# First layer of a four-layer image kernel: input rows in runs of 8192 bytes, single copies of shared rows, smaller steps, and row windows loaded for one group at a time instead of two

## What is computed

```python
def _gn(v, G=8, eps=1e-5):
    g = v.reshape(B_, G, C_ // G, H_, W_)
    ...
    return ((g - m) / jnp.sqrt(s + eps)).reshape(v.shape)
def _denoise_block(x, w1, b1, w2, b2, w3, b3, a, b, c):
    trip = _triplets(x)
    ...
    o = a * _conv_reflect(xf, w1, b1, 1, 2) + b * _conv_reflect(xf, w2, b2, 2, 4) + c * _conv_reflect(xf, w3, b3, 4, 8)
    return jnp.tanh(o).reshape(B, T, H, W)
y = _denoise_block(x, blk1_w1, ...)
z = _denoise_block(y, blk2_w1, ...)
return z
```

## Time and profile before

| | us |
|---|---|
| three runs | 5124.47, 5130.97, 5133.29 |
| the profiled execution | 5131.47 |
| its span | 5129.7 |
| TensorE busy | 4772.3 (93%) |
| VectorE busy | 4133.9 (81%) |
| ScalarE busy | 4039.3 (79%) |
| first group of layer 0 starts | 79.93 |
| last group of layer 0 starts | 2984.01 |

### The profile page before, as it was taken

One profiled execution on the slowest core, in us unless ns is written; L12 is line 12 of the kernel. 1 busy time (PEld: TensorE's weight loads), 2 busy tenths in 40 slices (PEclk: granted clock), 3 DMA queues, 4 the chain that ended last, 5 costly groups with the idle time before them and its releaser, 6 DMA issues. The chain is left out here.

```text
span 5129.7 us, 174298 instructions
## 1 busy us (share of the span) xinstructions
PE 4772.3 (93%) x74557; PEld 2805.2 (55%) x74557; DVE 4133.9 (81%) x7219; ACT 4039.3 (79%) x4023; POOL 1532.3 (30%) x1643
## 2 busy tenths in 40 slices
PE   4799999999999999999999979997776999999998
PEld 2344444445455795565566744434555566666665
DVE  5786786876867888888888868888999688888888
ACT  3576776776767888888888887876997799999897
POOL 0111111111113222222222100004776355555556
PEclk9899999999999999999999989998999999999999
DMA  8899899999978778788778769996886466666654
GB/s 220 224 246 261 249 266 255 248 259 252 247 211 236 221 217 240 230 221 248 220 229 243 216 235 324 323 325 236 308 309 247 114 150 153 150 153 150 153 150 119
DMA packets 501930, 1161.93 MB, mean 227 GB/s; under 512 B 59593, under 2 KB 60232, under 8 KB 468042
## 3 DMA queue, kind: packets, MB, share of 16 engines
q1 hardware_dynamic: 499000, 1148.40, 77.0%
q10 hardware_dynamic: 2162, 2.39, 0.2%
HBM read 678.71 MB, written 453.51 MB: 221 GB/s over the span
## 5 line engine op out<-in xcount | busy, mean ns | idle before, releaser
L702 PE MATMUL c_p<-c_w,wc 128*32 128x512 f16 x38912 | 2270.7, 380 | 53.5 <-DMA c_w<-xs 48.2
L702 PEld LDWEIGHTS c_p<-c_w,wc 128*32 128x32 f16 x38912 | 1239.7, 96 | 935.9 <-issue 42.7
L792 ACT ACTIVATE c<-c_w 64x2052 f16<-64x2052 f16 x512 | 984.7, 1923 | 87.3 <-DMA c_w<-xs 74.9
L778 ACT ACTIVATE c_t<-c_p,cbias,cscale 128x512 f32<-128x512 f32 x512 | 398.1, 777 | 541.2 <-PE c_p L702 538.6
L702 PE MATMUL c_p<-c_n,wc 128*32 128x512 f16 x8192 | 589.8, 381 | 20.4 <-DVE c_n L638 19.3
L1780 PE MATMUL f_P<-f_qh,f_wt 64*64 64x512 f16 x4608 | 545.7, 378 | 1.8 <-DVE f_t L1676 1.8
L1780 PE MATMUL f_P<-f_hl,f_wt 64*64 64x512 f16 x4608 | 545.3, 379 | 0.0
L884 POOL COPY c_y<-c_y 128x16 f16<-128x16 f16 x512 | 191.1, 401 | 1070.6 <-DVE c_y L609 1070.6
L794 ACT ACTIVATE c<-c_w 64x2052 f16<-64x2052 f16 x256 | 492.9, 1925 | 6.3
L1941 POOL TENSOR_TENSOR f_y<-f_y,f_x 128x512 f32<-128x512 f32 x256 | 330.8, 1292 | 449.4 <-DVE f_hl L1655 443.3
L1540 POOL TENSOR_TENSOR e_hl<-e_g,e_hl 128x2048 f16<-128x2048 f32 x63 | 257.2, 4083 | 608.4 <-ACT e_hl L1490 608.4
(11 more groups left out here) (275 smaller groups left out, 7681.6 us busy)
## 6 DMA issues: line engine op xcount, KB each, us to landing
d_x<-x SPq DMA_DIRECT2D x128, 1024.0 KB, 7.8
x<-d_x SPq DMA_DIRECT2D x128, 1024.0 KB, 5.1
ys<-c_y SPq DMA_DIRECT2D x576, 132.0 KB, 6.7
xs<-a_hl SPq DMA_DIRECT2D x70, 1056.0 KB, 10.1
a_x<-in_x SPq DMA_DIRECT2D x256, 256.0 KB, 7.1
a_x<-in_x SPq DMA_DIRECT2D x128, 512.0 KB, 5.0
x<-a_x SPq DMA_DIRECT2D x512, 128.0 KB, 5.3
f_x<-x SPq DMA_DIRECT2D x256, 256.0 KB
```

The costliest lines, as they stand in the source:

```text
L702: t = p.matmul(pg[32 * j:32 * j + 32, :], weights[:, var], source[:, j, at:at + NW], start=start, stop=stop, tile_position=(0, 32 * j))
L778: s.activation(tt_[n % 3][:, :], pp[:, n % 4, :], ACT.Tanh, bias=cbias[:, blk:blk + 1], scale=cscale[:, blk:blk + 1]).then_inc(c_act, 1)
L792: s.activation(twice[n % 2][64:128, :, PAD - 2:PAD - 1 + NW], w[0:64, :, PW + PAD + 1:PW + PAD + 2 + NW], ACT.Copy).then_inc(c_2b, 1)
```

## The change

- `load_x` brings one channel in one copy of 128 runs of 8192 bytes, so a partition now holds four neighbouring rows (before: four copies, runs of 2048 bytes). `store_xs` writes one channel per copy, as soon as that channel is ready.
- Pair 0 and pair 8 keep no second copies. Where a window needs them, `sources(p)` lists from where each slot is loaded: three sources for p = 0, two for p = 7, one for the others.
- `load` fills one group (four row sets) instead of two, with a semaphore for each group. The number of its copies in the first layer goes from 1008 to 2288.
- `v0`, `v3`, `hi`, `mirror`, `store_xs` work on one channel; the preparation of a pair takes six groups instead of four and begins two or three groups earlier. `p0` now follows a full group after the statistics, `p1_` sits early in its group.
- The weights of later layers are built in ten parts at groups 15 to 46 and two at 50 and 57.

The second sum has moved forward within its group, and both stand a group later against VectorE's steps. The core of the diff:

```diff
-        def n_xs(i):
-
-            return 16 * sum(2 + (r % 8 in (0, 7)) for r in range(i))
+        def inputs_stored(e, i):
+
+            e.wait_ge(a_sd, 32 * (i - (i > 1)))
+            if i > 1:
+                e.wait_ge(a_s1[0], 16)
+                e.wait_ge(a_s1[1], 16)
 
         def stored(e, u):
 
-            e.wait_ge(c_yd[u % 2], 16 * sum(8 + 4 * (place(r)[2] in (0, 7)) for r in range(u % 2, u, 2)))
+            e.wait_ge(c_yd[u % 2], 128 * (u // 2))
+
+        def sources(p):
+
+            outer = {0: [(0, (0,), 1, 0), (0, (1,), 0, 1)], 7: [(8, (0,), 8, 0), (8, (1,), 7, 1)]}
+            return outer.get(p, []) + [(p + 1, (0, 1), p + 1, 0)] * (p < 7)
 
         def at_edge(half, g):
 
-            return (half, g // 2) in ((0, 0), (1, 1))
+            return (half, g) in ((0, 0), (1, 3))
 
         def rows_in(e, u, g):
 
-            n = sum(1 + (place(r)[2] == 0) for r in range(u % 2, u + 1, 2))
-            e.wait_ge(c_ld[u % 2][g // 2], 16 * (3 + at_edge(u % 2, g)) * n)
+            n = sum(len(sources(place(r)[2])) for r in range(u % 2, u + 1, 2))
+            e.wait_ge(c_ld[u % 2][g], 16 * (3 + at_edge(u % 2, g)) * n)
 
...
-            return 64 * image + 4 + 7 * j + 2 * (i == 3) if i > 2 else -2
-
-        steps = {first_group(i) + z: (i, z) for i in range(2, NG) for z in range(4) if first_group(i) + z >= 0}
-        loads_x = {first_group(i - 2) + 4 + 2 * c: (i, c) for i in range(4, NG) for c in range(2)}
+            return 64 * image + 2 + 7 * j + (i == 3) if i > 2 else -3
+
+        steps = {first_group(i) + z: (i, z) for i in range(2, NG) for z in range(6) if first_group(i) + z >= 0}
+        parts_at = [15 + 7 * (z // 2) + 3 * (z % 2) for z in range(10)]
...
-                def v0(i):
-                    v.wait_ge(a_ld[i % 2], 128 * (i // 2 + 1))
-                    for j in range(8):
-                        v.bn_stats(ast[:, j, :], xin[i % 2][:, j // 4, 512 * (j % 4):512 * (j % 4) + 512]).then_inc(a_bn, 1)
-                    v.wait_ge(a_bn, 8 * (i + 1))
-                    mark["m", i] = ch.step(v, v.bn_aggr(am[:, 0, :], ast[:, :, :].rearrange("p a b -> p (a b)")))
+                def v0(i, c):
+                    v.wait_ge(a_ld[i % 2], 32 * (i // 2 + 1))
+                    for j in range(4):
+                        v.bn_stats(ast[:, 4 * c + j, :], xin[i % 2][:, c, 512 * j:512 * j + 512]).then_inc(a_bn, 1)
+                    if c:
+                        v.wait_ge(a_bn, 8 * (i + 1))
+                        mark["m", i] = ch.step(v, v.bn_aggr(am[:, 0, :], ast[:, :, :].rearrange("p a b -> p (a b)")))
 
                 def v1(i):
                     v.wait_ge(a_p, 2 * i + 1)
...
-                def channel_weights():
...
+                def channel_weights(part):
...
+                    if part == 0:
+                        v.wait_ge(w13_ld, 160)
+                        v.wait_ge(w13_p, 1)
+                        ch.step(v, v.tensor_copy(rp[:, :, :].rearrange("p j n -> p (j n)"), pq[:, 0:432]))
+                        ch.step(v, v.memset(qf[:, :, :], 0.0))
...
                     rows4 = buf[:, 4 * g:4 * g + 4]
+                    i, s = stage_of(n)
                     for di in (4, 0, 1, 7, 8):
+                        if s == 3 and di == 1:
+                            p1_(i)
                         for wl, xl in ((0, 0), (0, 1), (1, 0)):
                             four(wu[:, blk, wl, :, di], rows4, xl * PW + PAD + DX[di], start=(di, wl, xl) == (4, 0, 0))
-                    i, s = stage_of(n - 1)
-                    if s == 0:
+                    if s == 2:
                         p0(i)
-                    if s == 1:
...
                         i, st_ = stage_of(4 * u + g)
+                        if st_ == 3:
+                            root_step(s, a_v, mark["rt", i], a_rt, ve, sq)
                         if 4 * u + g + 1 < 8 * NU:
                             copies(4 * u + g + 1)
-                        if st_ == 2:
-                            root_step(s, a_v, mark["rt", i], a_rt, ve, sq)
-                        if (u, g) == (5, 2):
+                        if 4 * u + g == 50:
                             root_step(s, a_v, mark["sv"], w13_rt, c2b[:, 1:2], c2b[:, 2:3])
                         evict(u, g)
                         if u < NU:
                             high(u, g)
-                        if st_ == 2:
-                            hi(i)
+                        if st_ in (3, 4):
+                            hi(i, st_ - 3)
...
                 def load_x(i, channels=(0, 1)):
                     b, g = divmod(i, 8)
                     if i >= 2:
-                        e.wait_ge(a_lo, i - 1)
-                    for c, r in ((c, r) for c in channels for r in range(4)):
-                        e.dma_start(xin[i % 2][:, c, NW * r:NW * r + NW],
-                                    dram(x, ((b * NC + 2 * g + c) * NH + 16 * r) * NW, [[NW, 16], [64 * NW, 8], [1, NW]])).then_inc(a_ld[i % 2], 16)
-
-                def store_xs(i):
+                        e.wait_ge(a_lo, 2 * (i - 1))
+                    for c in channels:
+                        e.dma_start(xin[i % 2][:, c, :], dram(x, (b * NC + 2 * g + c) * NH * NW, [[4 * NW, 128], [1, 4 * NW]])).then_inc(a_ld[i % 2], 16)
+
+                def store_xs(i, c):
                     b, g = divmod(i, 8)
-                    e.wait_ge(a_pad, i + 1)
-                    for c, gp, slot in [(0, g, 1), (1, g + 1, 0)] + [(1, 0, 0)] * (g == 0) + [(0, 8, 1)] * (g == 7):
-                        e.dma_start(dram(xs, pair(b, gp, 0, slot), [[YP, 16], [64 * YP, 8], [16 * YP, 4], [1, RW]]),
-                                    halves_of(i)[c][:, :, :, :].rearrange("p r l w -> p r (l w)")).then_inc(a_sd, 16)
+                    e.wait_ge(a_pad, 2 * i + c + 1)
+                    e.dma_start(dram(xs, pair(b, g + c, 0, 1 - c), [[4 * YP, 128], [YP, 4], [1, RW]]),
+                                halves_of(i)[c][:, :, :, :].rearrange("p r l w -> p r (l w)")).then_inc(a_s1[c] if i == 1 else a_sd, 16)
 
                 def load(u, g):
 
                     blk, b, p, half = place(u)
-                    src, first, last = ys if blk else xs, (half, g) == (0, 0), (half, g) == (1, 2)
+                    src, first, last = ys if blk else xs, (half, g) == (0, 0), (half, g) == (1, 3)
                     if u >= 2:
-                        e.wait_ge(c_pe, 4 * (u - 2) + g + 2)
+                        e.wait_ge(c_pe, 4 * (u - 2) + g + 1)
                     elif u == 1 and g == 0:
                         e.wait_ge(a_v, mark["wc"])
                     if u < 2 and (first or last):
...
                         r = 16 * b + 2 * min(7, p + 1) + 2
                         stored(e, r)
                         stored(e, r + 1)
+                    elif u < 2:
+                        e.wait_ge(a_sd, 32)
+                        e.wait_ge(a_s1[0], 16)
                     else:
-                        e.wait_ge(a_sd, n_xs(8 * b + min(7, p + 1) + 1))
-                    f, n = int(first), 8 - first - last
-                    parts = [(0, 48, -4, f, n), (96, 8, -8, f, 8 - f), (112, 8, 20, 0, 8 - last)]
-                    parts += [(16, 40, 0, 0, 1)] * first + [(0, 40, -4, 7, 1)] * last
-                    for gp in (0, 1) if p == 0 else (p + 1,):
+                        inputs_stored(e, 8 * b + min(7, p + 1) + 1)
+                    f, n = int(first), 4 - first - last
+                    parts = [(0, 48, -4, f, n), (96, 8, -8, f, 4 - f), (112, 8, 20, 0, 4 - last)]
+                    parts += [(16, 40, 0, 0, 1)] * first + [(0, 40, -4, 3, 1)] * last
+                    for gp, slots, of, slot in sources(p):
                         for to, count, row, j, banks in parts:
-                            e.dma_start(win[half][to + gp % 2:to + 2 * count:2, 4 * g + j:4 * g + j + banks],
-                                        dram(src, pair(b, gp, 256 * half + 64 * g + 16 * j + row), [[RW, count], [16 * YP, banks], [1, RW]])).then_inc(c_ld[half][g // 2], 16)
+                            at = dram(src, pair(b, of, 256 * half + 64 * g + 16 * j + row, slot), [[(3 - len(slots)) * RW, count * len(slots) // 2], [16 * YP, banks], [1, RW]])
+                            first_p = to + gp % 2 + 2 * slots[0]
+                            e.dma_start(win[half][first_p:to + 2 * count:6 - 2 * len(slots), 4 * g + j:4 * g + j + banks], at).then_inc(c_ld[half][g], 16)
...
-                store_xs(0)
+                store_xs(0, 0)
+                store_xs(0, 1)
+                store_xs(1, 0)
                 load_x(2)
-                store_xs(1)
+                store_xs(1, 1)
                 for u in range(2):
-                    for g in (0, 2):
+                    for g in range(4):
                         load(u, g)
                 load_x(3)
...
-                        if s == 3:
-                            store_xs(i)
-                        if u + 2 < 2 * NU and not late and g % 2:
```

(55 more changed lines are left out.)

127 lines of the change are left out of this document (62 added, 65 removed).

## The result

The changed kernel takes 5208.35 us (median; 5198.64 to 5211.07) beside 5128.26 of the kernel before in the same session (5124.47 to 5133.29): ratio 1.0152, 95% interval 1.0135 to 1.017. The profiled execution took 5209.05 us, its span 5207.1. It is slower by some 80 us; forecast were 5151 and a range of 5045 to 5200.

The account below looks back on a forecast made before the run. TensorE was taken as the bound, busy 1387.8 of 1390 us in pass two. Terms -14 + 5.5 - 21 - 24 - 6 + 66 + 8 + 7 = +21.5, rounded to +20 on 5131.47, gave 5151 us; range 5045 to 5200.

Parts of the forecast that it names:

- the queue's terms: SyncE's queue, held about 0.70 us per window copy, lags at changes of image: +66, +8 and +7 us.
- rival A: The queue does not bind (copies hold it 0.55 us or less, or waits have slack): 5045 us, chance 0.25.
- Head, -14: Start of layer 0: earlier raw loads, stores and one-group windows start the first group at about 65.5 us, not 79.93.
- Groups 0 to 8, +5.5: Start of pass one: pair 3's raw load behind 78 window copies stops TensorE in group 5; group 8 near 139.5.
- Weights -21: Later layers' weights built in parts that fit beside a group, replacing two long VectorE blocks: -21 us.
- statistics -24: A full group between VectorE's result and `p0` removes TensorE's 24.2 us of waits for statistics: -24 us.
- waits for nothing shown -6: Weight loads waiting on "issue" near 1100 us, 11.4 us; about a tenth less traffic in pass one saves half: -6.
- Pass one: Late `ys` stores at three changes of image cost 11.5 us each, 34, against about 27 before: +7 us.
- Into pass two, +8: Passage into pass two (groups 248 to 260): the residual of group 264 comes some 6 us late, +8 us.
- Pass two, +66: Residual of an image's fourth unit late behind SyncE's queue: 22 us at each of three changes of image, +66.
- rival C: The queue binds harder, 0.736 us a copy, lag running into the next pair: 5200 to 5240; 0.10 with another rival.
- B: Rival: the queue binds half as hard, 0.65 us a copy, landing 3 us after issue: 5105 to 5130, chance 0.15.

Follow-up runs that it names:

- e3: The changed kernel, but pairs 0 and 8 store their second copies again (78 window copies at a change of image, loads still one group): 5031.22 us, ratio 0.9824.
- e5: e3 plus 52 empty copies per image and pass, issued behind the loads for p = 7 and p = 0: 5228.98 us, ratio 1.0215.
- e7: e3 with the second copy kept for pair 0 only, so 52 window copies for p = 7 and 52 for p = 0: 5069.23 us, ratio 0.9898.
- e10: The changed kernel with a group's `ys` store in pass one issued ahead of its window copies, not behind them: 5193.54 us, ratio 1.0137.
- e4: The kernel before with loads of one group instead of two as the only edit: 5133.33 us, ratio 1.0019.
- e1: The changed kernel with loads of two groups again everywhere: 5092.2 us, ratio 0.9943.

## Why the prediction was wrong

The step that failed is the size of the queue's terms, above all in pass one: +7 us was forecast for its changes of image and +42 came; in pass two it was +66 and +8 for 80 and 19.

**Right in mechanism and sign.** That a smaller copy holds the queue as long as a large one, that the lag builds up over p = 7 and p = 0, and that the residual in pass two and the `ys` stores in pass one are what is late, all stand in the trace, and e3, e5, e7 and e10 show it by adding and taking away. Without the queue's terms the prediction gave 5045 us (rival A's number); e3, in which no change of image stops TensorE, measured 5031.

**Head, -14.** Measured -16: the first c round at 70.72, 86.75 before.

**Groups 0 to 8, +5.5.** Measured +11: group 8 starts at 142.9, not 139.5. The stop in group 5 came as described and was longer:

```profile
127.05 0.58 PE L704 MATMUL a_p<-a_mv,ones 128*128 128x1 f32 x2 [25.51 <-DVE a_mv L450]
```

The raw load behind the windows was issued at 108.17, as the 78 copies took 57.66 us and not 55.

**Weights -21, statistics -24, waits for nothing shown -6.** The waits of the earlier trace rows for these are nearly gone: no stop over 1 us from 200 to 400 us; 4.7 us for statistics after 132 us, where 22.9 were; and from 1080 to 1170 us the weight loads of `c_p` no longer wait on "issue", where they did for 11.4.

**Pass one, the step that failed most: 34 us at the changes of image, measured 69.** Three things were wrong in "the last before group 68 is issued at 49 + 66 + 2 = 117 us from the start of the lag". Group 48 ends at 375.5, but the queue did not begin there:

```profile
376.41 1.14 SPq L962 DMA_DIRECT2D ys<-c_y  x2
380.85 0.56 SPq L916 DMA_DIRECT2D xs<-a_hl  x1
381.57 6.63 SPq L945 DMA_DIRECT2D c_w<-xs  x8
```

It waited 3.3 us for GpSimd's mirroring of the prepared channel, and started the windows 6 us late. Then it took 126 us, not 117, to the end of the store meant (506.72 + 1.14): p = 7 took 54.8 us, where the forecast has 49, and p = 0 71.5, where it has 66 and 2 for gaps. A group of nine copies takes 6.41 + 1.14 and 0.2 for its gaps, 7.75 in all, and 12 or 8 copies at the edges and two `xs` stores come on top. That is 132 us from the start of the lag. And only one stop was costed. There are two: the stores of the unit before those are late as well, which stops groups 66, 130 and 194 by 2.3, 8.3 and 9.9 us, ahead of groups 70, 134 and 198 with 11 to 12. The term of +7 against before is +42.

**Into pass two, +8: measured 19**, for the same reasons; it too has two stops (6.7 and 9.7 us).

**Pass two, +66: measured 80.** From 1868.38 to the end of the residual at 2003.59 the queue took 135.2 us, not 126.9: 56.9 for p = 7 (50.6 in the sum), 72.6 for p = 0 (68.8). The difference is stores of p = 7 that held it for 1.5 to 2.1 us instead of 1.26, its first eight copies (6.00 us), and 7.7 us for a group of nine copies where the sum has 7.56. The landing was 4.6 us (5.7 taken). The residual of the unit before was late too, so that the 25 to 28 us fell in several portions (3.5, 13.1 and 9.0 at the first change), and VectorE's waits for a residual reached 15.0 us at the longest, not over 15 at each change.

By stretch: the start 2 us better than forecast, pass one 37 worse and pass two 21 worse, together 56 of the 57 us missed. The result lies in rival C's band (5200 to 5240 us), but not by its price of 0.736 for a copy: nine took 6.41 us, 0.71 each, as the forecast had it; nor by late statistics (4.7 us of waits after 132 us). What the forecast lacked were the queue's wait ahead of the lag, the gaps and longer stores, and the second stop at each place. Three slips in the forecast's arithmetic change nothing in this: B's terms add up to 5096 us, not 5105 to 5130; 0.74 a copy gives a bound of +82, not +85; and the standstill of the kernel before is 140 us in both passes together.

**Not seen at all:** that two-group loads have a price of their own (the queue's 160.6 us of waiting in pass two of the kernel before), which the change removes. Without the rest of the change that is worth little: e4's pass two is only 4 us shorter.

## What to carry to other kernels

Count the issues per queue in each stretch, times what one holds the queue, against the time of the engine they feed; do it for the worst stretch and not for the mean, and add the queue's own waits, because here a lag of 7 us (by the sum) cost nothing, while 15 cost 40 to 55 and 33 cost 180 to 200. Splitting a copy costs a full issue; here writing a second copy of shared rows (one issue) saved three or more reads of them, so "remove redundant stores" was the part to leave out, and the rest of the change is worth 1.8% (e3). An issue moved forward in a queue can wait there for something that it had been hidden from: read what it waits for, before moving it.

## What the runs showed that was not expected

A copy of 256 bytes in all costs the queue 0.68 us at the median, a window copy of 396 KB (48 x 4 rows) 0.63, and one of half those rows (24 x 4, for a single slot) 0.78 to 0.83: the larger of the split copies of p = 7 and p = 0 move less and cost more. Stores of 64 rows and a channel of raw input are cheaper (0.60 at the median and 0.45 at least; 0.58). The landing of the stores follows how the loads are bunched: with one-group loads the store `x<-a_x` lands 2.8 us after its issue in the median,

```profile
x<-a_x SPq DMA_DIRECT2D x512, 128.0 KB, 2.8
```

and 5.3 us in the kernel before, at about the same rate of bytes (217 and 226 GB/s in pass two). e4, where only the loads differ from the kernel before, has 3.0 us, and e1 4.5.

TensorE's granted clock falls with the stops: in the change's windows it is 0.91 and 0.98 in pass one where e3 has 1.00 (means over its levels of 1.2 and 2.4 GHz), so a stop of 12 us costs one to two and a half us more in the group behind it (5.53 us for 76 matmuls that otherwise take 4.28).
